# A cross-attention and mixture-of-experts layer on one core: the passage from attention to the expert blocks, put in another order

## The chip, the cores and the metric

One Trainium2 chip, one of its cores. The metric is the device time of one execution in microseconds. The kernel before took 178.3 us (median of 3 runs, 177.25 to 179.37).

## The reference

Eight batches of 128 tokens with 128 features, all float32. Cut to what matters:

```python
x = x + tanh(g_xattn) * attention(layernorm(x), ctx, mask)      # 16 heads of 64, then Wo
h = layernorm(x)
shared = (silu(h @ sg.T) * (h @ su.T)) @ sd.T                   # 256 hidden units
scores, indices = top_k(sigmoid(h @ router_w.T + bias), 2)      # of 8 experts
scores = scores / sum(scores)
routed = sum over the 2 chosen experts of score * (silu(h @ gate) * (h @ up)) @ down
x = x + tanh(g_ffn) * (shared + routed)
```

## The kernel before, in words

The program of every engine is written out by hand, and semaphores order the engines among each other. Each engine takes its instructions in the order of the code, so a wait holds up all that stands behind it.

**Attention.** Batches go in four pairs. A head group `g` (0 to 15) is eight heads of one batch. TensorE computes `scores` into two banks; VectorE adds the mask and takes the row maxima in `mask_max` (L951, one instruction per head; its last argument is a generator whose steps are put in between the heads); ScalarE takes the exponentials (`exps`, L726); VectorE takes reciprocals of the sums (`recips`, L965); GpSimd multiplies (`normalise`, L1362, two quads of four heads); TensorE transposes (`transposes`, L391), ScalarE and VectorE copy the two banks out (`copy_pt`), TensorE multiplies by the values (`values`, L406), and the output goes through `wo` (`out_project`, L417; for the last batch in two halves, `out_project_half`, L426). GpSimd also splits the experts' weights into a rounded part and a rest (`split_expert`, L1368 and L1370), in gaps between its normalisings.

**Second norm and routing.** `add_attention` (L981) adds the projection to `x_sb`. `norm2_steps` is a generator of three steps (four for batch 7): statistics (L987), mean and variance with epsilon (L991, L993), and the normalised row `xrow` in two copies (L997; L1002 for batch 7, one copy at a time). Between the last two GpSimd takes the reciprocal root (`rstd_second`, L1350). Batches are routed in five turns `ROUTED` = (0,1), (2,3), (4,5), (6), (7), the last called `LAST`. A turn is: `x2_transposes` and `logits` on TensorE, `x2_copy`, `x2_hi` (rounding for the shared expert) and `route_exp` on ScalarE, `x2_lo`, `choose_steps` (sigmoid, top two, the one-hot rows `hot`, L1038) and `weight_steps` on VectorE, `ranks` on TensorE (how many tokens before this one chose the same expert), `place` (L1062, L1065: the slot in DRAM) on VectorE, `count_chosen` and `scatter` on GpSimd. `table_steps` on VectorE makes, in three stages, the table of which slots and which expert each block has; SyncE reads it to gather blocks, TensorE reads the expert's number (`block_expert`, L596, a load into a register).

**Blocks.** 23 blocks of 128 gathered rows each. For block `n`: TensorE transposes (L641), ScalarE rounds (`block_hi`, L865), VectorE subtracts (`block_lo`, L1265), TensorE multiplies by gate and up in three passes (L337 to L339), ScalarE takes SiLU (`block_silu`, L870), VectorE multiplies (`block_hidden`, L1270), TensorE transposes (L653) and multiplies by down (L662), ScalarE scales (`block_y`, L876), GpSimd scatters to DRAM (L1472). The shared expert's four units (`shared_pass`, L337 to L339) lie in between.

**The passage.** Between the last head group and block 0, TensorE runs the shared expert's first unit, the ranks of batch 6, two reads of the table, the transposes and logits of batch 7, and products of a tile of zeros that nobody reads (`stay_warm`, L600; each is two records in the trace). ScalarE runs `x2_split(LAST)`, `route_exp(LAST)` and then a SiLU of one column (L861), ahead of which the compiler puts the load of the table for SiLU; then `block_hi(0)`.

## Time and profile before

| | |
|---|---|
| median of 3 runs | 178.3 us (177.25 to 179.37) |
| the profiled execution | 177.18 us |
| its span | 175.4 us |
| TensorE busy | 160.6 us, 92% |
| VectorE busy | 131.4 us, 75% |
| ScalarE busy | 111.5 us, 64% |
| GpSimd busy | 110.0 us, 63% |

The span runs from the first to the last record of the profile; the time of the execution has some 1.8 us around it. A share of the whole span says little here, since the limits change from stage to stage: it is the idle time of one engine in one stretch, and what ended it, that tells what an edit there is worth. In a line of the instructions in order of time, the first number is the start in microseconds, the second the duration, then the engine, the line of the kernel, the operation, out<-in, the shapes, the count, and in brackets the idle time before it with what ended it.

### The profile page before, as it was taken

What the parts mean: (1) busy time and instruction counts of PE and PEld (TensorE: products, weight loads), DVE (VectorE), ACT (ScalarE), POOL (GpSimd) and SP (SyncE); (2) the same over time, 40 slices, a digit from 0 to 9 for tenths busy, and PEclk for the clock granted to TensorE, in tenths of its full rate; (3) what the DMA queues carried; (4) which work ended last, traced back from release to release, by engine and by line L of the source; (5) the groups of instructions that cost most, each with busy time, mean ns of one, the idle gap of its engine ahead of it and who ended that gap; (6) DMA issues with size and microseconds to landing.
All of it is one profiled execution on the core that took longest, in us unless ns stands there. A gap on an engine that the chain in (4) does not pass through costs nothing.

```text
span 175.4 us, 4620 instructions
## 1 busy us (share of the span) xinstructions
PE 160.6 (92%) x1415; PEld 140.1 (80%) x1415; DVE 131.4 (75%) x621; ACT 111.5 (64%) x427; POOL 110.0 (63%) x139
## 2 busy tenths in 40 slices
PE   7999889999997999999999999996699999999960
PEld 7887669997987998998998988884378788887860
DVE  2879988675999687898697999867794667776283
ACT  4566997775858873958873959732655666665400
POOL 3775799854868554588524687787156456666611
PEclk9999999999999999999999999999999999999998
DMA  5899996730000000000000000013124222211172
GB/s 158 263 374 351 415 396 266 294 124 0 19 2 0 19 2 4 15 32 27 24 4 0 15 21 17 15 50 85 38 65 114 67 67 77 58 51 41 55 241 90
DMA packets 11096, 17.35 MB, mean 99 GB/s; under 512 B 2075, under 2 KB 6945, under 8 KB 10944
## 3 DMA queue, kind: packets, MB, share of 16 engines
q1 hardware_dynamic: 9504, 14.59, 24.6%
q0 software_dynamic: 1280, 2.20, 3.8%
q8 instruction: 12, 0.20, 0.4%
q10 hardware_dynamic: 288, 0.26, 0.4%
q14 instruction: 12, 0.10, 0.2%
HBM read 9.99 MB, written 7.51 MB: 100 GB/s over the span
## 4 chain that ended last, share of the span: by engine, by line
PE 56%; POOL 11%; DVE 9%; issue 9%; ACT 9%; DMA 3%; SPq 1%; DVEq 0%; POOLq 0%
PE o_bank L406 7%; PE misc L417 6%; PE s_even L380 6%; POOL ys L1472 6%; PE pt L391 6%; ACT probs L726 5%; PE proj_q L337 3%; PE proj_k L337 3%; PE misc L487 3%; PE proj_q L338 3%; PE proj_q L339 3%; PE proj_k L339 3%; PE proj_k L338 2%; DMA probs<-ys 2%; PE pt L662 2%
## 5 line engine op out<-in xcount | busy, mean ns | idle before, releaser
L726 ACT ACTIVATE probs<-probs,negmax 128x128 f32<-128x128 f32 x128 | 49.8, 393 | 19.2 <-DVE negmax L951 19.1
L1362 POOL TENSOR_TENSOR probs<-probs,rinv 128x512 f32<-128x512 f32 x32 | 32.9, 1042 | 19.5 <-DVE rinv L965 19.2
L1472 POOL DMA_INDIRECT ys<-probsT,places x23 | 22.5, 979 | 14.7 <-ACT places L866 12.1
L726 ACT ACTIVATION_READ_ACCUMULATOR probs<-probs,negmax 128x1 f32 x128 | 24.3, 190 | 0.0
L1392 POOL DMA_INDIRECT xs<-xrow,slot x16 | 16.3, 1016 | 8.8 <-DVE slot L1065 4.9
L951 DVE CUSTOM_DVE_ANT_0 probs<-s_even,mask 128x128 f32<-128x128 f32 x64 | 18.1, 282 | 3.4 <-issue 3.2
L391 PE MATMUL pt<-ident_sb,probs 128*128 128x128 f32 x128 | 17.9, 278 | 1.9 <-POOL probs L1362 1.3
L380 PE MATMUL s_even<-kT,qT 64*128 64x128 f32 x128 | 18.4, 284 | 0.3 <-DVE negmax L951 0.3
L380 PE MATMUL s_odd<-kT,qT 64*128 64x128 f32 x128 | 18.5, 285 | 0.0
L380 PEld LDWEIGHTS s_even<-kT,qT 64*128 64x128 f32 x128 | 15.4, 187 | 3.5 <-issue 1.2
L951 DVE CUSTOM_DVE_ANT_0 probs<-s_odd,mask 128x128 f32<-128x128 f32 x64 | 18.1, 283 | 0.0
L391 PEld LDWEIGHTS pt<-ident_sb,probs 128*128 128x128 f32 x128 | 14.0, 140 | 4.4 <-POOL probs L1362 2.3
L406 PE MATMUL o_bank<-probsT,v 128*64 128x128 f32 x240 | 16.4, 279 | 0.9 <-ACT qT L715 0.8
L380 PEld LDWEIGHTS s_odd<-kT,qT 64*128 64x128 f32 x128 | 15.4, 187 | 0.0
L406 PEld LDWEIGHTS o_bank<-probsT,v 128*64 128x64 f32 x240 | 12.9, 136 | 2.8 <-ACT qT L715 1.2
L662 PE MATMUL pt<-down_sb,v 128*128 x92 | 14.5, 281 | 0.1
L417 PE MATMUL misc<-wo_sb,oT 128*128 128x128 f32 x112 | 13.9, 278 | 0.0
L417 PEld LDWEIGHTS misc<-wo_sb,oT 128*128 128x128 f32 x112 | 13.3, 192 | 0.8 <-issue 0.5
L876 ACT ACTIVATE probsT<-pt,xg 128x128 f32<-128x128 f32 x23 | 8.5, 368 | 8.4 <-PE pt L662 8.3
L662 PEld LDWEIGHTS pt<-down_sb,v 128*128 128x128 f32 x92 | 12.0, 191 | 1.1 <-issue 1.1
L951 DVE DVE_READ_ACCUMULATOR2_ANT negmax<- 128x1 f32 x128 | 10.5, 82 | 0.0
L969 DVE COPY probsT<-pt 128x512 f32<-128x512 f32 x14 | 9.4, 671 | 0.9 <-PE pt L391 0.8
(282 smaller groups left out, 461.4 us busy)
## 6 DMA issues: line engine op xcount, KB each, us to landing
xs<-pad SPq DMA_DIRECT2D x5, 858.0 KB, 6.9
xg<-xs SPq DMA_DIRECT2D x23, 66.0 KB, 1.9
down_sb<-down SPq DMA_DIRECT2D x1, 1152.0 KB, 10.2
probs<-ys SPq DMA_DIRECT2D x4, 256.0 KB, 4.1
gu_raw<-gu SPq DMA_DIRECT2D x3, 256.0 KB, 5.8
wk_raw<-wkT SPq DMA_DIRECT2D x2, 256.0 KB, 3.6
wq_raw<-wqT SPq DMA_DIRECT2D x2, 256.0 KB, 4.7
mask<-mask SPq DMA_DIRECT2D x8, 64.0 KB, 2.3
```

Of the source, the lines that this page charges most:

```text
L337: pe.matmul(dst, a_hi, b_hi, start=True, stop=False)
L339: return pe.matmul(dst, a_hi, b_lo, start=False, stop=True)
L380: mm = pe.matmul(s_bank[odd][:, j * P:(j + 1) * P], qT[rows, 4 * half + j, i * P:(i + 1) * P], kT[rows, 4 * half + j, i * P:(i + 1) * P], ...
L391: mm = pe.transpose(pt_bank[u][:, j * P:(j + 1) * P], probs[:, r, 4 * u + j, :], ident_sb[:])
L406: mm = pe.matmul(o_of.get(g, o_bank)[DK * odd:DK * (odd + 1), j * P:(j + 1) * P], v_sb[i][:, h * DK:(h + 1) * DK], probsT[:, half, 2 * j + ...
L417: mm = pe.matmul(misc[:, 0:P], oT[:, c // 4, c % 4, :], wo_sb[:, c, :], start=(c == 0), stop=(c == CHUNKS - 1))
L662: mm = pe.matmul(y_bank[:, 0:P], hidT[n % 2][:, c, :], down_sb[:, bass.ds(e * I_FFN + c * P, P)], start=(c == 0), stop=(c == 1))
L726: e = act.activation(probs[:, r, l, :], probs[:, r, l, :], ACT.Exp, bias=negmax[:, r, l:l + 1], scale=-1.0, accum_out=rowsum[:, r, l:l + 1])
L951: dve.tensor_tensor_reduce(probs[:, r, l, :], s_bank[l % 2][:, (l // 2) * P:(l // 2 + 1) * P], mask_sb[r // 2][:], -1.0, HUGE, ALU.add, AL ...
L1362: pool.tensor_tensor(quad, quad, rinv[:, r, 4 * u:4 * u + 4].unsqueeze(2).to_broadcast([P, 4, P]), ALU.mult).then_inc(norm_done, 1)
L1392: pool.indirect_dma_start(out=xs, out_offset=bass.IndirectOffsetOnAxis(ap=slot[:, b, k:k + 1], axis=0), in_=xrow[:, b, k, :], in_offset=No ...
L1472: pool.indirect_dma_start(out=ys, out_offset=bass.IndirectOffsetOnAxis(ap=places[:, n:n + 1].bitcast(U32), axis=0), in_=y_sb[n % IN_FLIGHT ...
```

## The change

Seven edits, most of them to the order in the passage:

- TensorE: the transposes of batch 6 (`x2_transposes(3)`) go between the halves of the last projection, its logits behind both. After the shared expert's first unit come the reads of the table, nine warming products, the transposes of batch 7, four warming products, its logits, the ranks of batch 6, and three warming products (before, one and five in all).
- ScalarE: `x2_hi(LAST)` goes behind `route_exp(LAST)`, and the one-column SiLU with its table load behind `block_hi(0)`.
- VectorE: in the first pass of the loop over pairs, `xrow` of batch 1 is not put in between the heads of `mask_max` but behind `copy_o(g + 4, 0)`.
- VectorE: `recips(15, 3, (1,))` goes ahead of the one-hot rows of turn 2.
- VectorE: both copies of `xrow` of batch 7 go right ahead of and right behind the one-hot row of batch 6, and `x2_lo(LAST)` behind `block_lo(0)`.
- GpSimd: `rstd_second(7)` goes ahead of `count_chosen(2)`.

```diff
--- before.py
+++ after.py
@@ -613,22 +613,23 @@
             transposes(15, 3)
             values(14, last, 2)
             values(15, last, 3)
+            out_project_half(B - 1, use + 1, 0)
             x2_transposes(3)
-            out_project_half(B - 1, use + 1, 0)
+            out_project_half(B - 1, use + 1, 1)
             logits(3)
-            out_project_half(B - 1, use + 1, 1)
             pe.wait_ge(gulo_ready, EXPERTS)
             pe.wait_ge(counts_read, 1)
             shared_pass(0, 0)
             shared_pass(0, 1)
+            pe.wait_ge(table_ready, 1)
+            experts = {n: block_expert(n) for n in range(2)}
+            stay_warm(9)
+            x2_transposes(LAST)
+            stay_warm(4)
+            logits(LAST)
             pe.wait_ge(ez_ready, 4)
             ranks(3)
-            pe.wait_ge(table_ready, 1)
-            experts = {n: block_expert(n) for n in range(2)}
-            x2_transposes(LAST)
-            stay_warm(1)
-            logits(LAST)
-            stay_warm(5)
+            stay_warm(3)
 
 
             def block_transpose(n):
@@ -856,9 +857,9 @@
             copy_o(15, 3)
             x2_split(3)
             route_exp(3)
-            x2_split(LAST)
+            x2_copy(LAST)
             route_exp(LAST)
-            act.activation(act_scratch[:], warm[:, 0:1], ACT.Silu)
+            x2_hi(LAST)
 
             def block_hi(n):
                 act.wait_ge(tx_done, n + 1)
@@ -876,6 +877,7 @@
                 act.activation(y_sb[n % IN_FLIGHT][:], y_bank[:, 0:P], ACT.Copy, scale=xg[n % IN_FLIGHT][:, P + 1:P + 2]).then_inc(y_ready, 1)
 
             block_hi(0)
+            act.activation(act_scratch[:], warm[:, 0:1], ACT.Silu)
             block_hi(1)
             block_silu(0)
             for n in range(BLOCKS):
@@ -1210,9 +1212,10 @@
                 add_attention(2 * p + 1, use + 1)
                 steps = norm2_steps(2 * p + 1, use + 1)
                 run(steps, 2)
-                mask_max(g + 6, p + 1, 2, after(4, run, steps, 1))
+                mask_max(g + 6, p + 1, 2, after(4, run, steps, 1) if p else iter(()))
                 recips(g + 6, 2, (0,))
                 copy_o(g + 4, 0)
+                finish(steps)
                 if p < PAIRS - 2:
                     recips(g + 6, 2, (1,))
 
@@ -1233,8 +1236,9 @@
             choice = choose_steps(2)
             run(choice, 2)
             recips(15, 3, (0,))
+            run(choice, 2)
+            recips(15, 3, (1,))
             finish(choice)
-            recips(15, 3, (1,))
             finish(weight_steps(2))
             place(2)
             add_attention(B - 2, use)
@@ -1250,13 +1254,12 @@
             norm = norm2_steps(B - 1, use + 1)
             run(norm, 2)
             choice = choose_steps(3)
-            run(choice, 3)
+            run(choice, 4)
+            run(norm, 1)
             finish(choice)
+            finish(norm)
             finish(weight_steps(3))
-            run(norm, 1)
             place(3)
-            finish(norm)
-            x2_lo(LAST)
             middle_table = table_steps(1)
             run(middle_table, 3)
 
@@ -1277,6 +1280,7 @@
             choice = choose_steps(LAST)
             run(choice, 3)
             block_lo(0)
+            x2_lo(LAST)
             finish(choice)
             finish(weight_steps(LAST))
             block_lo(1)
@@ -1461,8 +1465,8 @@
             scatter(2, 0, 1)
             rstd_second(B - 2)
             scatter(2, 1, 4)
+            rstd_second(B - 1)
             count_chosen(2)
-            rstd_second(B - 1)
             count_chosen(3)
             scatter(3)
             scatter(LAST)
```

TensorE in the passage, before; `L426` is a half of the last projection, `L443` transposes, `L454` and `L455` logits, `L596` reads of the table, `L600` warming products, `L470` to `L480` ranks, `L641` the block's transposes. An `x` counts instructions of the program.

```order
L426 MATMUL misc<-wo_sb,oT 128x128 x4
L337 MATMUL proj_q<-xn2T_hi,gu_hi 128x512
...
L480 MATMUL pt<-hot,before_bf 128x8 x2
L596 TENSOR_LOAD table x2
L443 MATMUL pt<-ident_sb,xrow 128x128
L600 MATMUL s_even<-warm 128x128
L454 MATMUL pt<-rows_sb,ident_sb 128x8
L455 MATMUL pt<-router_sb,x_raw 128x8
L600 MATMUL s_even<-warm 128x128 x5
L641 MATMUL o_bank<-ident_sb,xg 128x128 x2
```

And now, from the first half of the projection on:

```order
L426 MATMUL misc<-wo_sb,oT 128x128 x4
L443 MATMUL pt<-ident_sb,xrow 128x128
L426 MATMUL misc<-wo_sb,oT 128x128 x4
L454 MATMUL pt<-rows_sb,ident_sb 128x8
L455 MATMUL pt<-router_sb,x_raw 128x8
L337 MATMUL proj_q<-xn2T_hi,gu_hi 128x512
...
L596 TENSOR_LOAD table x2
L600 MATMUL s_even<-warm 128x128 x9
L443 MATMUL pt<-ident_sb,xrow 128x128
L600 MATMUL s_even<-warm 128x128 x4
L454 MATMUL pt<-rows_sb,ident_sb 128x8
L455 MATMUL pt<-router_sb,x_raw 128x8
```

The ranks of batch 6, with three warming products behind them, follow these; they stood ahead of the reads of the table before. Batch 6's transposes stood ahead of the first half of the projection.

VectorE around the heads of group 6, before (`ISA` is the mask-and-maximum instruction of one head and the reading of its maximum; the row of batch 1 is `L997`):

```order
L951 ISA negmax 128x1
L997 TENSOR_SCALAR xrow<-x_sb,moments,rstd 128x2x128
L951 ISA probs,negmax<-s_even,mask 128x128
...
L965 RECIPROCAL rinv<-rowsum 128x4
L973 COPY oT<-o_bank 128x512
L965 RECIPROCAL rinv<-rowsum 128x4
L969 COPY probsT<-pt 128x512
```

And now:

```order
L953 ISA negmax 128x1
L967 RECIPROCAL rinv<-rowsum 128x4
L975 COPY oT<-o_bank 128x512
L999 TENSOR_SCALAR xrow<-x_sb,moments,rstd 128x2x128
L967 RECIPROCAL rinv<-rowsum 128x4
L971 COPY probsT<-pt 128x512
```

The row left the heads and stands between the copy of the output and the second reciprocal.

ScalarE ahead of block 0, before:

```order
L756 CAST xn2T_hi<-x_raw 128x128
L768 ACTIVATE ez<-pt 128x8
L861 ACT_TABLE_LOAD
L861 ACTIVATE act_scratch<-warm 128x1
L865 CAST xg_hi<-o_bank 128x128
L866 COPY places<-xg 128x1
```

And now:

```order
L769 ACTIVATE ez<-pt 128x8
L757 CAST xn2T_hi<-x_raw 128x128
L866 CAST xg_hi<-o_bank 128x128
L867 COPY places<-xg 128x1
L880 ACT_TABLE_LOAD
L880 ACTIVATE act_scratch<-warm 128x1
```

The exponential of batch 7's logits and the rounding of block 0 moved ahead, the table load behind both.

## Rows read from the trace of the kernel before

**Rows 1.** Stretches: us, busy PE, PEld, DVE, ACT, POOL (records), PEclk, DMA, GB/s.

```profile
50.00:55.00 5.00, 3.91 (x43) 3.55 (x43) 4.58 (x18) 4.05 (x18) 3.63 (x5) 1.00 0.01 2
55.00:111.00 56.00, 55.81 (x585) 50.46 (x582) 46.86 (x269) 41.41 (x173) 35.88 (x45) 1.00 0.05 15
140.00:162.00 22.00, 21.76 (x146) 18.86 (x146) 15.30 (x46) 14.22 (x56) 14.32 (x15) 1.00 0.22 61
```

**Rows 2.** Instructions in order of time, 50 to 55 us.

```profile
50.32 1.50 DVE L997 TENSOR_SCALAR xrow<-x_sb,moments,rstd 128x256 f32<-128x256 f32 x1
50.38 1.28 POOL L1370 TENSOR_TENSOR gu_lo<-wq_raw,gu_hi 128x512 fp32r<-128x512 f32 x1
...
50.97 0.39 ACT L726 ACTIVATE probs<-probs,negmax 128x128 f32<-128x128 f32 x1
...
51.74 0.28 DVE L951 CUSTOM_DVE_ANT_0 probs<-s_even,mask 128x128 f32<-128x128 f32 x1
...
52.06 0.40 ACT L726 ACTIVATE probs<-probs,negmax 128x128 f32<-128x128 f32 x1 [0.60 <-DVE negmax L951]
...
54.75 0.51 PE L406 MATMUL o_bank<-probsT,v 128*64 128x128 f32 x5 [0.79 <-ACT qT L715]
```

**Rows 3.** Instructions in order of time, 109 to 114 us.

```profile
109.62 1.05 POOL L1362 TENSOR_TENSOR probs<-probs,rinv 128x512 f32<-128x512 f32 x1
109.63 0.39 ACT L726 ACTIVATE probs<-probs,negmax 128x128 f32<-128x128 f32 x1
109.67 1.07 DVE L1038 TENSOR_TENSOR hot<-rows_sb,chosen_at 128x32 bf16<-128x32 f32 x1
...
110.84 0.17 PE L470 MATMUL proj_q<-hotsum,ones_bf 128*128 128x8 bf16 x1
...
110.90 1.04 POOL L1362 TENSOR_TENSOR probs<-probs,rinv 128x512 f32<-128x512 f32 x1 [0.23 <-DVE rinv L965]
...
112.00 0.65 PE L391 MATMUL pt<-ident_sb,probs 128*128 128x128 f32 x4 [0.20 <-POOL probs L1362]
```

**Rows 4.** Instructions in order of time, 114 to 127 us.

```profile
114.85 0.33 PE L443 MATMUL pt<-ident_sb,xrow 128*128 128x128 f32 x1 [0.30 <-DVE xrow L997]
...
115.92 0.29 PE L454 MATMUL pt<-rows_sb,ident_sb 128*128 128x8 f32 x2
...
116.28 1.14 PE L426 MATMUL misc<-wo_sb,oT 128*128 128x128 f32 x8
...
117.18 0.48 PE L337 MATMUL proj_q<-xn2T_hi,gu_hi 128*128 128x512 f32 x1
...
120.70 0.30 PE L443 MATMUL pt<-ident_sb,xrow 128*128 128x128 f32 x1 [0.76 <-DVE xrow L1002]
...
121.82 1.36 PE L600 MATMUL s_even<-warm 128*128 128x128 f32 x10
121.87 0.22 DVE L1074 SCALAR_TENSOR_TENSOR full<-pt,rows_sb 128x64 f32<-128x64 f32 x1
...
122.19 1.28 ACT L861 ACT_TABLE_LOAD   x1
...
123.02 0.27 PE L641 MATMUL o_bank<-ident_sb,xg 128*128 128x128 f32 x1
...
123.88 0.29 DVE L1265 TENSOR_TENSOR xg_lo<-o_bank,xg_hi 128x128 fp32r<-128x128 f32 x1 [0.70 <-ACT xg_hi L865]
...
124.65 0.27 ACT L865 CAST xg_hi<-o_bank 128x128 fp32r<-128x128 f32 x1 [0.72 <-PE o_bank L641]
...
124.96 0.28 DVE L1265 TENSOR_TENSOR xg_lo<-o_bank,xg_hi 128x128 fp32r<-128x128 f32 x1
...
126.79 0.41 DVE L1270 TENSOR_TENSOR kT<-kT,s_even 128x256 f32<-128x256 f32 x1
```

**Rows 5.** TensorE's table loads, line 596: duration in ns, smallest, median, largest.

```profile
L596 PEldq TENSOR_LOAD <-table x23: 298/304/489, 119.7 to 158.2; - x23
```

**Rows 6.** The chain of work that ended last: start us, us, what.

```profile
120.34 0.36 issue
```

## The prediction

> **What bounds the kernel now.** I read the busy time by stretches first, to see which engine has no idle time where. [rows 1] shows three stretches: TensorE has work for 55.81 of the 56 us from 55 to 111, and for 21.76 of the 22 us from 140 to 162, at a granted clock of 1.00 (2.4 GHz); in the 5 us from 50 to 55 it works only 3.91. So it is the bound of the attention loop and of the block loop, and time is to be had only where it stands idle: 1.09 us around 52, and the passage from the last attention heads to the first expert block, 111 to 127.
>
> Second, the order of time around 52 [rows 2]. VectorE's mask-and-maximum pass over eight heads feeds ScalarE's exponentials. After the fourth head the hook puts in the normalised row of batch 1 (L997). It takes 1.50 us, because GpSimd runs the split of an expert's weights (L1370, 1.28) just then; it ends 0.15 after GpSimd's. ScalarE's fifth exponential waits 0.60, and TensorE's values product at 54.75 stands behind all this with 0.79 idle (the other 0.30 is the scores product just before, which waits for the same maxima).
>
> Third, the passage [rows 3, 4]. TensorE goes from the transposes of head group 15 (112.00) through values and the last projection to the shared expert's product (117.18), the transposes of batch 7 (120.70), warming products (121.82, ten records: a product over 128x128 float32 takes two) and the first block's transposes (123.02). ScalarE then loads the SiLU table (1.28) ahead of the first block's rounding, so VectorE's subtraction for block 0 waits 0.70 (123.88). From there VectorE is the bound: it goes without a gap to the first block's hidden product at 126.79, which TensorE waits for. After that TensorE is the bound to the end, and GpSimd's scatters follow each block. An earlier start of the blocks moves the end by as much.
>
> **The change, part by part.** All times are on the clock of the old trace.
>
> *Row of batch 1 moved behind the copy of the attention output.* The eight maxima then run on (one takes 0.28, an exponential 0.39, so they stay ahead), and the fifth exponential starts when the fourth ends: 50.97 + 0.39 = 51.36 instead of 52.06 [rows 2], so 0.70 sooner. The reciprocal that ends this group, VectorE's copy behind it and the values product all come 0.70 sooner: 54.05. The row itself meets GpSimd again: the first quad's normalising starts about 51.7, where the split ends, takes 1.04, and holds the row until about 52.9. ScalarE's last exponential ends at 51.36 + 4 x 0.39 = 52.9 too, and the reciprocal behind the row waits for that until 53.0, so the row is hidden, by 0.1. Bounds: 0, if the row holds the reciprocal as long as the stall did, and -1.09, all of the idle time. I take **-0.70**. In the next stretch TensorE has no idle time [rows 1], so the gain stays until 111. For the later pairs of batches the emitted order is the same.
>
> *Reciprocal of head group 15 ahead of the one-hot row (choice of batches 4 and 5).* In [rows 3] the one-hot comparison (L1038) takes 1.07, as long as GpSimd's normalising beside it (1.05); the reciprocal comes behind it, so GpSimd's next quad starts at 110.90 after an idle 0.23. The last exponential began at 109.63 and ends at 110.02, so the reciprocal can go at about 110.15, and GpSimd runs on at 110.69: **-0.21** on TensorE's transposes at 112.00. But the one-hot row now waits with a second quad right behind the first. Both ends: it gets in between them (-0.21), or it waits for the second too (+0.83, the first rival). I take the first, for both long VectorE rows of [rows 2, 3] end within 0.15 of the end of one GpSimd instruction.
>
> [rows 3] shows an operation of VectorE with two SBUF operands standing still for the length of GpSimd's (1.07 beside 1.05). The Trainium skill ("SBUF — State Buffer", section "SBUF: two separate sides") says that the port pair they share is an exclusive lock, held for a whole instruction by whichever starts first. By that rule the trace agrees for one instruction; it doesn't say who is first when both wait, and no row here shows it.
>
> *Batch 6's transposes between the halves of the last projection, logits behind both.* Before, the first half stood behind the transposes, which waited for the row of batch 6 until 114.85 with 0.30 idle, and the logits stood ahead of the second half, at 116.28 [rows 4]. Now half 0 follows the values at about 114.25 (114.55 less the 0.21 above and the time by which weights load ahead), takes 8 records at 0.1125 = 0.90, the transposes 0.17 (what they took ahead of half 0), and half 1 starts at 115.33: 0.95 sooner. VectorE still has 0.2 of subtractions to end, so the residual of batch 7 gains 0.9. The logits (0.36, from 115.92 to 116.28) now lie between half 1 and the shared expert's product: 115.33 + 0.90 + 0.36 = 116.59 against 117.18, **0.59 sooner**.
>
> *Two table loads of TensorE, more warming.* The shared pass takes 6 x 0.235 and 0.06 (117.18 to 118.65); now it ends at 118.06. Two table loads follow, 0.49 for the first and 0.30 for the second [rows 5]. Before, they came behind short products, began at 119.7 and kept the transposes of batch 7 from 120.34, when their row was ready, to 120.70 [rows 6]. I take them at nothing here: in the block loop fifteen such loads lie in a stretch in which TensorE idles 0.24 in all [rows 1, 5], so its queue reads ahead under products in flight, and the last shared products cover 0.8. Uncovered they cost 1.03 (second rival). Then nine warming products, 18 x 0.1115 = 2.01: transposes of batch 7 at 120.07 (120.70 before; their row is ready by 120.34 - 0.9 = 119.4, and sooner if GpSimd's reciprocal root, now ahead of its additions for the counts, comes earlier). Four more, 0.13 + 0.89: logits at 121.09, 0.26 before their old start (121.82 less four records, 121.35). Ranks behind them at 121.56 to 121.71, three warming products 0.67: **first block's transposes at 122.38, 0.64 sooner**.
>
> *VectorE in between.* The slots of batch 6 now wait for the late ranks, so its table work, which began at 121.87, begins at 121.71 + 0.2 + 0.3 = 122.2, 0.33 later. Its 1.30 of work up to the maximum (123.17) ends at 123.5. The old order stood idle until 123.88, so block 0's subtraction comes **0.4 sooner** in spite of that.
>
> *ScalarE.* The first block's rounding goes ahead of the table load: 122.38 + 0.3 = 122.70. The load and its dummy then take 1.5 and block 1's rounding starts at 124.45 instead of 124.65. VectorE has the subtraction of batch 7, moved here, as 0.2 more, and reaches block 1's (124.96 before) at 124.76, just when ScalarE is done. So the hidden product comes at 126.59: **-0.20**. Bounds: -0.4, if the added 0.2 vanishes, and +0.83, the sum of what the rivals may take.
>
> The Trainium skill ("ScalarE: Activation LUTs", section "What ACT_TABLE_LOAD costs") puts 1.38 us of drain beside a load of 1.28. The row of the load has 1.28, and the next rounding starts 1.4 after it began, so the trace does not show the drain. If it came now, behind a busy pipe, the sum would be +0.5 instead of -0.9; that is the last rival.
>
> *Sum.* -0.70 - 0.20 = -0.90. The profiled execution took 177.18 (its span is 175.4, and 1.8 lie around it), so 176.3; the median of the runs is 178.3, 1.1 above that execution, so **177.4**.
>
> **The rivals.**
> 1. *The one-hot row loses the port.* It ends at 111.79 instead of 110.73. TensorE's ranks (110.84 in [rows 3]) stand ahead of the transposes of group 15: 111.85 + 0.32 + 0.45 = 112.62 for those that I put at 111.79, +0.83 on all that follows. Sum -0.08: 178.2. For it: both wait for the end of the same instruction, and nothing in the program orders them. Against it: the long rows that the trace has end with the first instruction they met, though there GpSimd had no second one waiting.
> 2. *The loads are not covered; the slower side.* TensorE's queue has nothing in flight when it reaches the table loads, and thirty-two warming records wait behind them. 0.49 + 0.30 and some 0.24 between and behind them (119.7 to 120.70) = 1.03 on the transposes of batch 7, the slots and the first block. It decides from 0.9 on: sum +0.13, 178.4, slower than before. For it: that is just what they did at 119.7 to 120.7 [rows 5, 6]. Against it: the products in front are long ones now.
> 3. *The stall only moves.* The row of batch 1 holds the reciprocal behind it as long as it held the maxima, and the first term is nothing: -0.20, 178.1. For it: it meets GpSimd at its new place too. Against it: ScalarE is later.
> 4. *The drain shows.* Block 1's rounding 1.38 later: +0.48, 178.8. Against it: the row.
>
> **How the numbers follow.** Forecast 0.60, first rival 0.18, second 0.09, third 0.10, last 0.03. Within 1% (1.8 us, about what a measurement of this kernel can tell from no change) lie all of these. For more than 1% faster the gain would have to be twice my sum, or the runs would have to scatter that way: the three shown span 177.25 to 179.37, so I give it 0.11; slower by 1% needs two rivals together, 0.03. The range takes -1.09 and -0.4 at one end (176.8) and the last rival but a little at the other (178.8), each with half a microsecond for the scatter of a median, cut on the slow side where little chance lies: 176.3 to 178.9.
>
> **What would show it right or wrong.** Around 52: no row of VectorE between the fourth and fifth heads, ScalarE's eight exponentials without a gap, values at 54.05. At 110: reciprocal at 110.15 - 0.7, and the one-hot row ending with the first quad, not the second. The transposes of batch 7 at about 119.4 on the new clock, with no gap of TensorE ahead of the warming products. The rounding of block 0 ahead of the table load, VectorE without idle time ahead of block 0's subtraction, and the first hidden product 0.9 sooner, at 125.9. I am wrong if the scores still wait at 52, if the one-hot row lasts over 1.3, if TensorE idles at 118, or if TensorE idles more in the block loop than the 0.24 of before.

## The result and the profile after

The changed kernel takes 176.94 us (median of 18 executions, 176.58 to 177.86), the kernel before, beside it on the same chip, 178.53 us (18 executions, 176.96 to 179.66): ratio 0.9927, 95% interval 0.9899 to 0.9955. That is 0.7% less: the interval leaves out 1, so it is a small gain, but it lies inside the 1% that I took as the bound of what a measurement can tell, and the time lies inside the range. The profiled execution went from 177.18 to 176.62 us, its span from 175.4 to 174.8. So the median fell by 1.59 us and the profiled execution by 0.56 us; the sum had said 0.90 for both. The experiments explain most of this gap between the two.

The first value product after the stall, beside [rows 2], and the engines ahead of it, instructions of the changed kernel in order of time (start us, us, engine, line, operation, in brackets the idle time before it with what ended it):

```profile
51.27 0.39 ACT L727 ACTIVATE probs<-probs,negmax 128x128 f32<-128x128 f32 x1
...
51.65 1.04 POOL L1366 TENSOR_TENSOR probs<-probs,rinv 128x512 f32<-128x512 f32 x1
...
52.07 0.77 DVE L999 TENSOR_SCALAR xrow<-x_sb,moments,rstd 128x256 f32<-128x256 f32 x1
52.94 0.18 DVE L967 RECIPROCAL rinv<-rowsum 128x4 f32<-128x4 f32 x1
...
53.95 1.09 PE L406 MATMUL o_bank<-probsT,v 128*64 128x128 f32 x16 [0.45 <-ACT qT L716]
```

The fifth exponential no longer waits, the row of batch 1 (now L999) lies behind the heads, and the value product comes at 53.95 instead of 54.75. This profile lies 0.09 earlier than the old one before the stall already, so the edit gave 0.71. To keep such shifts out, I read each trace below from this value product on: the time from it to the first hidden product was 126.79 - 54.75 = 72.04 us before.

The one-hot row, beside [rows 3], same view:

```profile
108.77 2.04 POOL L1366 TENSOR_TENSOR probs<-probs,rinv 128x512 f32<-128x512 f32 x2
...
109.30 0.18 DVE L967 RECIPROCAL rinv<-rowsum 128x4 f32<-128x4 f32 x1 [0.52 <-ACT probs L727]
109.47 1.40 DVE L1040 TENSOR_TENSOR hot<-rows_sb,chosen_at 128x32 bf16<-128x32 f32 x1
```

GpSimd goes from one quad to the next without a gap, and the one-hot row lasts 1.40 us instead of 1.07: it ends at 110.87, with the second quad (108.77 + 2.04 = 110.81), not between the two. TensorE's ranks stand ahead of the transposes in the queue, so all eight transposes of this group start late, at 111.31; the second four then start at about 111.76 (an estimate, at 0.11 for each transpose). On the old clock (plus 0.80) that is 112.56 instead of 112.00.

The passage, beside [rows 4], TensorE, VectorE and ScalarE:

```profile
114.22 1.16 PE L426 MATMUL misc<-wo_sb,oT 128*128 128x128 f32 x8
115.22 0.27 PE L443 MATMUL pt<-ident_sb,xrow 128*128 128x128 f32 x1
...
117.82 0.39 PE L339 MATMUL proj_k<-xn2T_lo,gu_hi 128*128 128x512 f32 x1
118.05 2.17 PE L600 MATMUL s_even<-warm 128*128 128x128 f32 x18
...
118.67 0.34 DVE L1004 TENSOR_SCALAR xrow<-x_sb,moments,rstd 128x128 f32<-128x128 f32 x1
...
120.06 0.27 PE L443 MATMUL pt<-ident_sb,xrow 128*128 128x128 f32 x1
...
121.75 0.17 DVE L1064 TENSOR_TENSOR at<-hot,pt 128x16 f32<-128x16 bf16 x1 [2.22 <-PE pt L480]
...
122.33 0.27 PE L642 MATMUL o_bank<-ident_sb,xg 128*128 128x128 f32 x1
...
123.01 1.28 ACT L880 ACT_TABLE_LOAD   x1
...
123.27 0.27 DVE L1268 TENSOR_TENSOR xg_lo<-o_bank,xg_hi 128x128 fp32r<-128x128 f32 x1
...
124.41 0.25 ACT L866 CAST xg_hi<-o_bank 128x128 fp32r<-128x128 f32 x1
...
126.53 0.41 DVE L1273 TENSOR_TENSOR kT<-kT,s_even 128x256 f32<-128x256 f32 x1
```

The warming products start 0.23 behind the last shared product: TensorE's table loads are hidden. The transposes of batch 7 start at 120.06 although their row was done at 118.67 + 0.34 = 119.01; a full microsecond of warming lies between. VectorE then stands idle for 2.22 us, waiting for the counts of batch 6 that TensorE has behind all of this. The hidden product comes 126.53 - 53.95 = 72.58 us behind the value product: the passage is 0.54 us slower than before, and the moved row's 0.71 pays for it. That leaves 0.17 of the forecast 0.90; the hidden product, which I wanted at 125.9, comes at 126.53.

The end of the two profiles doesn't speak for the change either. GpSimd's last scatter starts at 165.19 before and at 165.04 now, 0.15 sooner; most of the 0.56 between the two executions comes behind it, in the wait for the gathered rows that are added up at the end:

```profile
170.28 1.50 POOL L1478 TENSOR_TENSOR probs<-probs 128x256 f32<-128x256 f32 x2 [4.12 <-DMA probs<-ys]
```

```profile
169.53 1.69 POOL L1482 TENSOR_TENSOR probs<-probs 128x256 f32<-128x256 f32 x2 [3.51 <-DMA probs<-ys]
```

The first line is of the kernel before, the second of the changed kernel. A second profile of the changed kernel (`e11` below) has 4.32 for the same wait: it differs by more between executions of one kernel than between these two, and no gain can be read from it.

Stretches of the changed kernel, TensorE alone (us, busy, granted clock, DMA share, GB/s), which the experiments come back to:

```profile
118.00:122.00 4.00, 4.00 (x42) 1.00 0.30 73
122.00:127.00 5.00, 2.91 (x21) 1.00 0.18 51
```

### The profile page after: what moved, and what is told of

It is laid out like the page before. It is cut to its first block, busy times and chain, and to the rows that moved or that the text cites. A ratio compares the mean times of both kernels' runs of the same rounds, so it can differ in the third digit from the quotient of the medians.

```text
span 174.8 us, 4660 instructions
## 1 busy us (share of the span) xinstructions
PE 161.2 (92%) x1435; PEld 141.3 (81%) x1435; DVE 130.7 (75%) x621; ACT 111.1 (64%) x427; POOL 109.9 (63%) x139
## 4 chain that ended last, share of the span: by engine, by line
PE 62%; ACT 10%; POOL 9%; DVE 9%; issue 6%; DMA 2%; DVEq 0%; SPq 0%; POOLq 0%
PE pt L663 6%; ACT probs L727 5%; PE misc L417 5%; POOL probs L1366 5%; PE pt L391 5%; PE o_bank L406 5%; PE s_even L380 4%; PE proj_q L337 3%; PE proj_k L337 2%; PE proj_k L339 2%; PE proj_k L338 2%; PE proj_q L338 2%; PE proj_q L339 2%; PE s_even L600 2%; POOL xs L1396 2%
## 5 line engine op out<-in xcount | busy, mean ns | idle before, releaser
L733 ACT COPY probsT<-pt 128x512 f32<-128x512 f32 x16 | 9.2, 572 | 1.8 <-PE pt L391 1.8
```

Of the source, the lines that this page charges most:

```text
L733: act.copy(probsT[:, r % 2, 0:4, :].rearrange("p h q -> p (h q)"), pt_bank[0][:]).then_inc(pt0_free, 1)
```

## The experiments

Each run lists the mean granted clock of TensorE over the execution. This turned out to matter, so the table sorts by it; "held" means a mean of 0.984 or more. "us" is the median of the executions in that group; "to hidden" is the time from the first value product behind the stall to the first hidden product in the profiled execution. There are three batches of runs, each on one chip, with its own runs of the kernel before on that chip; single executions of over 190 us, one each beside or in `e0`, `e2` and `e4`, are left out of the groups.

| run | median, us | ratio | clock 0.984 or more | 0.971 to 0.980 | below 0.971 | to hidden, us |
|---|---|---|---|---|---|---|
| before, batch 1 | 178.03 | | 9 at 176.99 | 14 at 178.02 | 10 at 178.99 | 72.04 (profile ahead of the prediction) |
| `e0` before again | 178.08 | 0.9971 [0.9935, 1.0008] | 4 at 177.19 | 5 at 178.12 | 2 at 180.95 | 73.24, clock lost |
| `e1` row alone | 177.77 | 0.9969 [0.9926, 1.0012] | 3 at 176.09 | 4 at 177.63 | 5 at 178.49 | 73.53, clock lost |
| `e2` without the row | 177.83 | 0.9989 [0.9957, 1.0022] | all | | | 72.58 |
| `e3` one-hot row first | 176.23 | 0.9917 [0.9887, 0.9947] | all | | | 72.00 |
| before, batch 2 | 177.93 | | 7 at 177.45 | 7 at 178.22 | 2 at 179.20 | |
| `e4` warming alone | 177.93 | 0.9994 [0.9967, 1.0021] | all | | | 72.12 |
| `e5` sparse warming | 175.90 | 0.9896 [0.9848, 0.9944] | all | | | 71.47 |
| `e6` shorter warming | 175.64 | 0.9876 [0.9832, 0.9919] | all | | | 71.14 |
| `e7` shorter still | 175.52 | 0.9873 [0.9826, 0.9920] | all | | | 71.02 |
| before, batch 3 | 177.97 | | 12 at 177.20 | 6 at 178.50 | 5 at 179.25 | |
| `e8` reciprocal alone | 178.67 | 1.0036 [0.9996, 1.0076] | 1 at 177.37 | 8 at 178.63 | 3 at 180.09 | 72.54, clock lost |
| `e9` both losses undone | 175.58 | 0.9848 [0.9797, 0.9899] | all | | | 71.15 |
| `e10` ranks first | 175.89 | 0.9879 [0.9823, 0.9936] | all | | | 71.25 |
| `e11` after again | 177.20 | 0.9962 [0.9922, 1.0002] | all | | | 72.60 |

Two limits of these columns. The mean over an execution doesn't show a short fall of the clock: the profiled executions of `e7` (mean 0.985) and `e10` (0.989) stand under "all", but their traces show some 3 us at a granted clock of 0.50 where the first blocks begin; `e0` has some 7 there and `e1` some 10 (estimates, from the granted clock in steps of 1 us). And the time to the hidden product leaves out what follows it. Where that matters I give the time from the same value product to the start of GpSimd's last scatter as well: 110.44 us in the kernel before (165.19 - 54.75), 111.09 and, in `e11`, 111.14 in the changed kernel. By this mark the passage and what follows it lose 0.65 to 0.70, as much as the row gains.

**`e0`: the kernel before, unchanged.**

> The kernel before once more, unchanged, for a second profile and to see how its runs spread: those known lie in two groups, about 177.3 and about 179.1 us, while all runs of the changed kernel lie between 176.6 and 177.9. Theory A (the spread is in the stretches that the change touches, most likely a wait between VectorE and GpSimd that some runs have and others don't): a run of the upper group, if the profile catches one, shows 1 to 2 us more between 49 and 127 us. Theory B (the spread lies in the loads at the start or at the end): the stretch between is the same to 0.2 us. Ratio 1.000 in both.

Its profile caught what the one ahead of the prediction had not. The page's line of the granted clock, in tenths over 40 slices of the span:

```profile
PEclk9999999999999999999999999997599999999999
```

The stretches of TensorE (us, busy, granted clock, DMA share, GB/s):

```profile
118.00:120.00 2.00, 0.90 (x9) 1.00 0.10 34
120.00:122.00 2.00, 1.38 (x8) 0.88 0.40 99
122.00:124.00 2.00, 2.00 (x11) 0.50 0.49 137
124.00:126.00 2.00, 1.23 (x5) 0.50 0.00 0
126.00:128.00 2.00, 2.00 (x12) 0.50 0.00 0
128.00:130.00 2.00, 2.00 (x10) 0.91 0.37 105
```

And TensorE's instructions there:

```profile
121.72 2.48 PE L600 MATMUL s_even<-warm 128*128 128x128 f32 x10
123.99 0.42 PE L641 MATMUL o_bank<-ident_sb,xg 128*128 128x128 f32 x1
```

From 118 to 122 TensorE has work for 2.28 of 4 us, and from 122 to 128 it runs at a granted clock of 0.50, the lower level of 1.2 GHz. The five warming products take 2.48 us where [rows 4] has 1.36, and the hidden product comes 1.20 us later. This happened in 24 of the 33 executions of the kernel before in this batch (1.0 or 2.0 us dearer), and in 44 of 72 over the three; the profile ahead of the prediction was of the others.

**`e1`: the kernel before with the row of batch 1 moved, and nothing else.**

```diff
-                mask_max(g + 6, p + 1, 2, after(4, run, steps, 1))
+                mask_max(g + 6, p + 1, 2, after(4, run, steps, 1) if p else iter(()))
                 recips(g + 6, 2, (0,))
                 copy_o(g + 4, 0)
+                finish(steps)
```

> The kernel before with one edit alone: the row of batch 1 behind the copy of the attention output. Theory A (this edit is the gain and worth 0.7 us, as in the two profiles): ratio 0.996, values product 0.7 us sooner at 54, and the 0.7 us kept to the end. Theory B (the edit also takes away what puts most runs of the kernel before 1.8 us up): ratio 0.992 to 0.993, as the whole change has, and runs in one group. Theory C (the passage to the blocks is where the gain is): ratio 0.999 or more.

The medians can't tell it from the kernel before, for in 9 of 12 executions the clock falls here too. Among those that held it the time is 176.09 against 176.99 us, 0.90 less, but these are three. The clearer reading comes from the pair without the fall:

**`e2`: the changed kernel with this one edit undone** (the diff of `e1` backwards).

> The changed kernel with the row of batch 1 put back in between the heads; all other edits kept. Theory A: the passage is worth nothing by itself, since the one-hot row now waits for two quads (first rival, +0.8 against the forecast of -0.2, less what the bound of VectorE hides): ratio 0.999 to 1.002. Theory C: ratio 0.993 to 0.996. The stall at 50 us comes back, 1.5 us for the row.

Here and in the changed kernel the time to the hidden product is the same, 72.58 us, and only what lies ahead of the value product differs: the row is worth 0.71 by the traces and, by the medians (177.83 on this batch's chip, 176.94 and 177.20 elsewhere, so a difference of chips may be in it), 0.6 to 0.9. With the clock held the rest of the change is a loss, on one chip: 177.75 us against 176.99.

**`e3`: the changed kernel with the one-hot row ahead of the reciprocal again.**

```diff
             recips(15, 3, (0,))
-            run(choice, 2)
-            recips(15, 3, (1,))
             finish(choice)
+            recips(15, 3, (1,))
```

> The changed kernel with one edit undone: the one-hot row of turn 2 again ahead of the second reciprocal of head group 15. Theory A (the one-hot row lost to the second quad, and that cost 0.8 us of what the passage gains): it takes 1.05 us instead of 1.40, TensorE's 0.89 us of idle time ahead of the ranks is gone, the first block's hidden product comes 0.5 to 0.6 us sooner than in the changed kernel, and the ratio to the kernel before is 0.989 to 0.990. Theory B (VectorE or something else is the bound of the passage, so TensorE's wait was hidden): the hidden product within 0.1 us of the changed kernel's.

Instructions in order of time:

```profile
108.72 1.07 DVE L1040 TENSOR_TENSOR hot<-rows_sb,chosen_at 128x32 bf16<-128x32 f32 x1
...
109.96 1.04 POOL L1365 TENSOR_TENSOR probs<-probs,rinv 128x512 f32<-128x512 f32 x1 [0.23 <-DVE rinv L967]
...
111.05 0.66 PE L391 MATMUL pt<-ident_sb,probs 128*128 128x128 f32 x4 [0.20 <-POOL probs L1365]
...
121.07 0.17 DVE L1064 TENSOR_TENSOR at<-hot,pt 128x16 f32<-128x16 bf16 x1 [1.92 <-PE pt L480]
```

The one-hot row is back at 1.07, GpSimd has its gap of 0.23 again and gains by it: the second quad's transposes start at 111.05 (111.76 in the changed kernel, whose profile runs 0.10 later). Everything behind is 0.6 sooner, and the time is 176.23 us. The changed kernel did not run in this batch. `e2` did, and the 1.5 us between `e2` (177.75) and `e3` are the row's 0.7 and some 0.8 for the one-hot row. VectorE's wait of 1.92 us for the counts is still there.

**`e4`: the kernel before with nothing but additional warming products.**

```diff
+            stay_warm(4)
             pe.wait_ge(ez_ready, 4)
             ranks(3)
+            stay_warm(3)
```

> The kernel before with nothing of the change but its additional warming products, put where TensorE waits anyway: a stay_warm(4) ahead of the wait of ranks(3) and a stay_warm(3) behind ranks(3). Theory (the added products keep TensorE's granted clock at 2.4 GHz behind the passage, and this makes most of the measured difference of the medians): every execution lists a mean granted clock of 0.989 or more, the stretch 122 to 127 us shows 1.00 where the kernel before showed 0.50, and the time falls by 0.5 to 1.0% to about 177.0 us, with the spread of the runs cut to some 0.5 us. Rival (the clock falls for a reason that lies outside the kernel, and the products only take queue time): the executions fall into the same three groups of clock as before's and the ratio is 0.998 to 1.003.

All 12 executions held the clock, at 0.990 or more, against 7 of 16 of the kernel before beside them: the products do keep it. But the time did not fall: 177.93 us is the median of the kernel before too, and 0.48 above its seven executions that held the clock. The traces agree up to the last block (counted from the value product, hidden product 0.08 later, last scatter 0.13 later), and the last wait, GpSimd's for the gathered rows, is 4.63 us against 4.12. That wait ran from 3.5 to 4.6 us over the profiles of this study without an order that I could see, so why holding the clock was worth nothing here stays open.

**`e5`: the changed kernel with as few warming products as before.**

```diff
-            stay_warm(9)
             x2_transposes(LAST)
-            stay_warm(4)
+            stay_warm(1)
             logits(LAST)
             pe.wait_ge(ez_ready, 4)
             ranks(3)
-            stay_warm(3)
+            stay_warm(5)
```

> The changed kernel with as few warming products as before, in its own order: none ahead of the last batch's transposes, one ahead of its choice product, five behind ranks(3). Theory (the products hold the clock, not the new order): part of the executions list a mean clock of 0.96 to 0.98, and the time spreads from 176.2 us (clock held) to 179 us, median near 177.8. Rival (the new order by itself fills the idle stretch of TensorE at 118 us well enough): all clocks stay at 0.989 or more, and the time is 176.0 to 177.0 us, since the nine products ahead of the transposes no longer delay anything.

The rival stands: all six executions are at 0.988 or more without the products, and the profiled one shows 1.00 throughout the passage. Instructions of TensorE and VectorE in order of time:

```profile
118.74 0.40 PE L339 MATMUL proj_k<-xn2T_lo,gu_hi 128*128 128x512 f32 x1
119.64 0.33 PE L443 MATMUL pt<-ident_sb,xrow 128*128 128x128 f32 x1 [0.50 <-DVE xrow L1003]
...
121.12 0.17 DVE L1063 TENSOR_TENSOR at<-hot,pt 128x16 f32<-128x16 bf16 x1 [0.64 <-PE pt L480]
```

TensorE now waits 0.50 for the row instead of delaying it, VectorE's wait for the counts falls from 2.22 to 0.64, and the passage is 1.11 us shorter. (This profile runs some 0.9 later from the start; hence the time to the hidden product.)

**`e6` and `e7`: one-hot row first, and less warming.** Against `e3`, the nine products become four; then the four behind the transposes become two as well.

```diff
-            stay_warm(9)
+            stay_warm(4)
             x2_transposes(LAST)
-            stay_warm(4)        (e7 only)
+            stay_warm(2)        (e7 only)
```

> The changed kernel with the one-hot row put ahead of the last reciprocal again, and the first of the new warming calls cut from nine products to four. Theory (at 121 us VectorE waits 1.9 us for the counts of the third quad, and these stand in TensorE's queue behind the warming products; 5 of them at some 0.12 us go): the counts come 0.6 us sooner in the queue, and the end falls by 0.5 to 1.1 us against the run with the one-hot row first, to 175.1 to 175.7 us, ratio near 0.986, if the clock is held. Rival (the row of the last batch, which comes from ScalarE and VectorE, ends last there, not the queue): no change against that run, 176.2 us. Second rival (fewer products let the clock fall): clocks of 0.97, median of 177.5 us or more.

> As the run before, with the second warming call cut from four products to two as well. Theory: up to 0.25 us more if the queue still ends last ahead of the counts, nothing if VectorE's copy of the transposes ends last; the point is where the clock stops being held: with six products ahead of ranks(3) instead of thirteen some executions may list 0.97, and then the median is above that of the run before. Expected 175.0 to 176.3 us.

`e6` came as expected: 0.86 us less to the hidden product than `e3`, at 175.64 us. `e7` takes 0.12 more off that time, at 175.52 us, and all 12 executions are at 0.984 or more. But in `e7` a stretch of the profile shows the fall (columns as in [rows 1], the clock is the 0.71):

```profile
122.00:127.00 5.00, 4.11 (x19) 2.65 (x19) 4.37 (x26) 3.04 (x11) 2.73 (x3) 0.71 0.28 81
```

Read in steps of 1 us, the clock is at 1.00 until 124, between 0.50 and 0.54 from 124 to 127, and back at 1.00 from 128; in the microsecond from 121 to 122, ahead of it, TensorE had work for 0.16. Most of this lies behind the first hidden product (124.96). The last scatter comes 109.81 us after the value product in `e7` and 109.54 in `e6`: what `e7` was ahead is lost again, and 0.27 more. The medians, six executions each, can't tell the two apart.

**`e8`: the kernel before with the reciprocal alone ahead of the one-hot row.**

```diff
             recips(15, 3, (0,))
+            run(choice, 2)
+            recips(15, 3, (1,))
             finish(choice)
-            recips(15, 3, (1,))
```

> The kernel before with one edit of the change alone: the reciprocal of the 15th group's second half put ahead of the one-hot row. Theory (the one-hot row then meets two GpSimd instructions in a row and is held through both; measured in the changed kernel as 1.40 us instead of 1.07 us and 0.6 us later for the multiplication behind it): the one-hot row takes 1.40 us, the time between the first value product and the first hidden product grows from 72.04 us by 0.5 to 0.7 us, and executions with the clock held take 177.9 to 178.3 us where those of the kernel before take 177.0 to 177.5 us; ratio 1.001 to 1.005. Rival (the earlier reciprocal frees GpSimd's scaling sooner, as the prediction had it): the one-hot row stays at 1.07 us, time from the first value product to the hidden product 71.8 us, ratio 0.998.

The one-hot row in order of time:

```profile
110.43 1.40 DVE L1038 TENSOR_TENSOR hot<-rows_sb,chosen_at 128x32 bf16<-128x32 f32 x1
```

The 1.40 us are there again, so the order alone makes them. What they cost in the old order can't be read from the time: only 1 of 12 executions held the clock, and 177.37 us for it is below the 177.9 to 178.3 that I expected. The 72.54 us to the hidden product, 0.50 more than before, are no reading of it either, since the clock was at 0.50 from about 123 on. In the trace the transposes of batch 7 come 0.23 later, counted from the value product (121.11 - 54.93 against 120.70 - 54.75), for there TensorE waits for their row in any case.

**`e9`: both losses undone,** the edits of `e3` and `e5` together.

> The changed kernel with both of its losses taken back: the one-hot row first, and the warming products as sparse as in the kernel before (none, one, five). Theory (the two losses are separate, 0.58 us for the one-hot row and 1.1 us for the thirteen products in the queue ahead of the last counts): from the first value product to the first hidden product 70.9 us, where the changed kernel has 72.58 us; time 175.2 to 175.6 us, ratio 0.984 to 0.987, clocks 0.985 or more since the new order alone keeps TensorE busy enough. Rival (both sit in one another's shadow, since VectorE ends last in either case): 71.4 us and 175.9 us. Second rival (the clock falls without the products now that TensorE gets ahead of VectorE): clocks of 0.97 and a median above 176 us.

Instructions in order of time, and the stretch from 118 to 122 of TensorE:

```profile
119.05 0.33 PE L443 MATMUL pt<-ident_sb,xrow 128*128 128x128 f32 x1 [0.78 <-DVE xrow L1003]
...
120.53 0.17 DVE L1063 TENSOR_TENSOR at<-hot,pt 128x16 f32<-128x16 bf16 x1 [0.64 <-PE pt L480]
```

```profile
118.00:122.00 4.00, 2.90 (x26) 1.00 0.26 64
```

175.58 us, 1.62 less than the changed kernel beside it, and 71.15 us to the hidden product: between theory (70.9) and first rival (71.4). The two losses overlap in part: the one-hot row is worth 0.58 with the long warming (`e3`) and 0.32 without (`e5` to `e9`). The last scatter comes 109.59 us after the value product, 1.55 sooner than in `e11`. TensorE idles 1.1 us in the stretch, the profile shows the clock at 1.00 behind it, and all six executions are at 0.989 or more.

**`e10`: the ranks of batch 6 ahead of the logits of batch 7,** from `e7`.

```diff
             x2_transposes(LAST)
-            stay_warm(2)
-            logits(LAST)
             pe.wait_ge(ez_ready, 4)
             ranks(3)
+            stay_warm(1)
+            logits(LAST)
             stay_warm(3)
```

> An attempt at a better version: one-hot row first, four warming products ahead of the last transposes, then ranks(3) directly behind these transposes, one warming product, and the choice product of the last batch behind that. In the run with the shortest warming VectorE waited 0.64 us at 119.9 us for the counts, which stood in the queue behind two warming calls and the choice product. Theory: this wait goes, the slots of the third quad come 0.5 us sooner, and the first hidden product 0.3 to 0.5 us sooner: 175.0 us, ratio 0.984. Rival (the choice product is late instead, and with it the last batch's one-hot row and the hidden product behind it on VectorE): no change, 175.5 us.

Instructions in order of time, and the stretch behind them of TensorE:

```profile
119.30 0.17 DVE L1064 TENSOR_TENSOR at<-hot,pt 128x16 f32<-128x16 bf16 x1
...
120.96 0.33 PE L642 MATMUL o_bank<-ident_sb,xg 128*128 128x128 f32 x1 [0.25 <-DMA xg<-xs]
```

```profile
122.00:127.00 5.00, 4.81 (x20) 0.66 0.28 79
```

VectorE's wait is gone, as the theory had it, 0.6 us sooner. But the first block's transposes now wait for the gathered rows themselves, the clock falls to a mean of 0.66 in this stretch, and the hidden product comes 0.23 us later than in `e7`. The last scatter, at 109.64 us after the value product, is level with that of `e6` (109.54) and `e9` (109.59): no gain, by two causes that this run doesn't separate. The refinement failed.

**`e11`: the changed kernel again, beside `e8` to `e10`.**

> The changed kernel unchanged, once more, on the chip of these runs, so that all four stand side by side: 176.9 us, ratio 0.993, every clock 0.989 or more, 72.5 us from the first value product to the first hidden product. Rival (its margin over the runs with fewer warming products was one of chips): within 0.3 us of the run with the sparse warming.

By both times a copy of the first result: 72.60 us to the hidden product, and executions all at 0.987 or more. The kernel before, beside it, held the clock in 12 of 23 executions this time, at 177.20 us: with the clock held in both, the change is worth nothing here, as the traces have it up to the last scatter. The difference to `e9`, 1.6 us, is not one of chips.

## Why the prediction was right or wrong

The number held (176.94 in place of 177.4, and no difference of more than 1%), but two of its steps were wrong in opposite directions, and that it held is in part luck: by the traces the change gives 0.17 of the 0.90 in the sum, and the kernel before carried a loss of clock that the sum doesn't contain.

- **The row of batch 1, -0.70: right.** 0.71 by the trace, 0.75 in the times when `e3` is compared with the kernel before at held clock on the same chip (176.23 and 176.99), where the time to the hidden product has hardly changed (72.00 against 72.04). The step by which the row hides under ScalarE's last exponentials holds too: row until 52.84, exponentials until 52.81, reciprocal at 52.94.
- **The reciprocal ahead of the one-hot row, -0.21: wrong; the first rival happened.** The step that failed is "it gets in between them", and the sign that I had set for it, a row of over 1.3, came: 1.40. Of two instructions that waited for the end of the same GpSimd instruction, GpSimd's next one went first. I had reasoned from the two long VectorE rows of [rows 2, 3], but behind neither of them stood a second GpSimd instruction that was ready. The rival's numbers fit: it put the late transposes at 112.62 on the old clock, they came at 112.56, so the -0.21 was +0.56. `e3` takes the edit back and gains 0.58 to the hidden product and 0.7 us in the median (of another batch); `e8` makes the 1.40 us with this edit alone.
- **The halves of the projection, 0.59 sooner: right, given the first rival.** In `e3`, which has neither the 0.21 nor the loss, the shared product comes 0.38 sooner, counted from the value product; that is 0.59 less 0.21. The transposes lie between the halves at 115.22.
- **TensorE's table loads covered, and warming of 2.01: right.** 118.05 to 120.06 is 2.01 us, and nothing stands between the last shared product and the warming. The second rival fell.
- **The first block's transposes 0.64 sooner, the hidden product 0.20: right once the lost port is put in.** Without the 0.21, the steps give 0.43 and nothing; `e3` shows 0.48 and 0.04. With the lost port 0.54 is lost instead.
- **The drain: not seen.** The load takes 1.28, the next rounding begins 1.40 after it (123.01, 124.41).
- **The price of the warming: not asked.** I had the products in the sum, but asked neither what they bought nor what the same order would do without them. I saw that the row of batch 7 would be ready 0.7 before its transposes. `e5` shows the price, 1.11 us to the hidden product, and `e9` that both losses together cost 1.6 us of a change that could have won 2.4 us against the median of the kernel before (ratio 0.985), or 1.6 against its executions at held clock.
- **"The median is 1.1 above that execution": wrong as a step.** I carried this 1.1 over to the new kernel as scatter. It goes with the clock: the executions of the kernel before lie at 177.0, 178.0 and 179.0 us (first batch) by their mean clock. The kernel before lost it in the passage in most executions, and the one profiled had not; no row of one profile at 1.00 shows this, but the three times shown (177.25 to 179.37, beside a profiled 177.18) were a reason to ask. None of the 30 executions of the changed kernel is below 0.987. So the medians differ by 1.59 on the first chip, by 0.77 on the chip of `e11`, where the kernel before lost it less often, and there by nothing when both hold it (177.20 both). For the first chip the clocks of the kernel before are not on record; six of its 18 executions took 176.96 to 177.38 us, the other twelve 177.63 to 179.66. One run speaks against so simple an account, and it stays unexplained: `e4` held the clock and was no faster.

What keeps off the long falls, those of some 7 and 10 us, is shown from two sides. With the old order, the kernels with sparse warming (`e0`, `e1`, `e8`) held the clock in 8 of 35 executions, and `e4`, which only adds products, in 12 of 12. With the new order all 30 executions of `e5`, `e6`, `e7`, `e9` and `e10`, with six to eleven products in place of the sixteen (the kernel before has six), were at 0.984 or more. Either one is enough for that; the added products weren't needed for it. Short falls are another matter: of the five profiles of the new order with fewer products, `e7` (nine products) and `e10` (eight) have one, `e5`, `e6` and `e9` (six, eleven, six) have none, and neither do the four profiles of the new order with all the products, nor `e4`. Whether the products keep off the short falls is not shown, and which edit of the new order keeps off the long ones was not tried.

In the traces the clock is at 1.00 or 0.50, with means of stretches between, and the executions of one program lie in three groups. The Trainium skill ("TensorE: Matmul & The Clock Gate", section "Part 1: The HAM clock gate") has the clock at one of two levels by how busy TensorE has been recently, and warns that the same kernel may meet the change at another place in each run. The runs agree with both.

## What to carry to other kernels

Ahead of a sum from one profile, ask whether its granted clock is that of the median execution: a spread of 2 us between executions, with a stretch where TensorE idles, is a term of the sum and not scatter. An operation of VectorE that GpSimd holds up, as the one-hot row here, belongs in a gap between two GpSimd instructions, and what releases the second of them belongs behind it, not ahead. Warming products ahead of an instruction whose data is ready delay it: five fewer of them, 1.1 us of TensorE's time (ten records of 0.11), brought the hidden product 0.86 us forward (`e6`). Reorder the work first, then add the fewest that keep the clock, and read it in many executions, not in one.

## What the hardware showed that I had not expected

- A one-hot row of VectorE that became ready while GpSimd was in the first of two back-to-back instructions lasted 1.40 us, to the end of the second (109.47 to 110.87 against 110.81), in all five profiles with this order, and 1.07 us, to the end of the first, in the nine others, where GpSimd's second wasn't ready. The Trainium skill ("SBUF — State Buffer", section "SBUF: two separate sides") has the port pair locked for a whole instruction by whichever starts first. The runs add that here GpSimd, which was in the first of its two instructions, went on with the second ahead of the waiting row.
- One program ran at three mean clocks: the kernel before had 0.99 to 1.00, about 0.973 and about 0.966, at 177.0, 178.0 and 179.0 us. In `e0` the clock was at 0.50 for some 7 us behind a stretch in which TensorE worked 2.28 of 4 us; the first profile of the same kernel has the same 2.28 of 4 us and stays at 1.00. The profile of `e9`, with 2.90 of the same 4 us, stays there too.
- A fall of the clock can hide from a mark that lies ahead of it: `e7`, with 0.71 in 122 to 127, is the fastest of all by its time to the hidden product (71.02 us), and by its last scatter 0.27 us behind `e6`, which has 1.00 there.
